# Inverting the softmax sums of the last node phase by logarithm, exponential and one Newton step instead of a division

## The chip, the cores and the metric

The kernel runs on one core of one Trainium2 chip. The time is device microseconds of one execution; the median of three runs stands for a kernel. The profile is of one more execution, taken by the hardware profiler. Engines are TensorE (PE, and PEld for its weight loads), VectorE (DVE), ScalarE (ACT), GpSimd (POOL) and SyncE (SP, which here issues DMAs).

## What is computed

A graph of 6250 nodes with 128 features passes through four layers (attention, a GIN-like layer, an equivariant layer, attention by feature), each followed by a residual sum and a layer norm. The change lies behind the last one, of which this is the core:

```python
a = f_src[src] + f_dst[dst]
e = jnp.where(a >= 0, a, NEG_SLOPE * a)
sa = _edge_softmax(e, dst, n)            # exp(e - max) / sum over the edges of a node
m = f_v[src] * sa
rst = jax.ops.segment_sum(m, dst, num_segments=n)
...
x = _layernorm(x + rst, axis=-1)         # (x - mean) / sqrt(var + 1e-5)
```

The division by the sum is the same for all edges of a node, so the kernel adds up exponentials and weighted exponentials and divides once per node and feature.

## The kernel before, in words

Nodes lie in 49 tiles of 128 (partition = node in the tile). `x` holds the features [128, 49, 128], `acc` the accumulators [128, 49, 384]. The program is a row of phases: a projection, then four times an edge phase (`edges0` to `edges3`: gather rows of both ends, compute messages, add them up by matrix multiplications with selection matrices, add to `acc`) and a node phase (`after0` to `after3`). A barrier over all engines stands between phases.

Behind `edges3`, `acc[:, tile, 0:128]` holds the sums of exponentials and `acc[:, tile, 128:256]` the weighted sums. `acc[:, tile, 256:384]`, which the program calls `side(tile)`, held one end's features for `edges3` and is not read any more.

`after3` (L736) handles 13 blocks of four tiles (128x512 numbers an instruction), the last one being a single tile. For a block it does:
- ScalarE, L749: the sum plus 1e-30, by an Identity with a bias column `tiny`, into `s`
- VectorE, L753: reciprocal of that, into `z`
- GpSimd, L757 and L760: times the weighted sums, plus `x`
- `layernorm` (L482): VectorE takes statistics of the four tiles (L487), aggregates them (L490), adds eps (L473, a tensor_scalar on 128x4 numbers); ScalarE takes the root (L477); VectorE the reciprocal (L480) and minus mean times that (L493); ScalarE writes the four tiles of the output by an activation with scale and bias (L500)
- SyncE, L766 and L769: the block's write-out.

Five streams work in turn, each with its own tiles and semaphores: stream k has blocks k, k+5, k+10. `node_phase` (L523) fixes the order of the instructions on every engine when the program is built: each step of a stream yields the engine it needs and a weight, and the loop always takes the step that could start first by those weights, the older block first among equals. On the chip the engines follow these lists in order and wait for each other by semaphores. `k.enter` makes the first instruction of a block on an engine wait for all that the stream's block before has done; `also` is a further chain of steps beside the streams, which `after3` doesn't use yet.

Of the kernel before, what the change touches and what calls it, by code (L numbers as in the profile page):

```python
# [15 lines left out]
P = 128  # L16
N_NODES = 6250
N_EDGES = 106250
D = 128
BLOCK = 4  # L20
STREAMS = 4
X_TILES = 12
N_TILES = -(-N_NODES // P)
# [8 lines left out]
N_BLOCKS = -(-N_TILES // BLOCK)  # L32
# [17 lines left out]
ALU = mybir.AluOpType  # L50
ACT = mybir.ActivationFunctionType
# [31 lines left out]
def wait(engine, *marks):  # L83

    last = {}
    for counter, at in marks:
        last[counter] = max(at, last.get(counter, 0))
    for counter, at in last.items():
        engine.wait_ge(counter.sem, counter.round * counter.per + (counter.base + at))
# [62 lines left out]
def build(nc, a):  # L152
    PE, V, A, G, SP = nc.tensor, nc.vector, nc.scalar, nc.gpsimd, nc.sync
# [26 lines left out]
    def sb(ctx, name, shape, dt=F32):  # L180
        return ctx.enter_context(nc.sbuf_tensor(name, shape, dt))


    x = sb(root, "x", [P, N_TILES, D])
    acc = sb(root, "acc", [P, N_TILES, ACC_W])
# [16 lines left out]
    def side(tiles):  # L202

        return acc[:, tiles, SIDE:SIDE + D]
# [7 lines left out]
    def counters(ctx):  # L212
        return lambda name, by=1: Counter(ctx.sem(name), by)
# [187 lines left out]
    def sliced(t, k):  # L401

        return t[:, 0:k.size]
# [119 lines left out]
    def node_phase(tag, make, n_streams=STREAMS, also=None, begin=0.0):  # L523

        with Phase(nc, tag) as ctx:
            def blocks(k, steps):
                for b in range(k.number, N_BLOCKS, n_streams):
                    k.start(b)  # L530
                    yield from steps()

            def age(s):
                return chained[s].first if chained[s] else -1

            streams = [Stream(ctx, s, n_streams) for s in range(n_streams)]
            chained = [None] * bool(also) + streams
            closing = []
            chains = ([also(ctx, closing)] if also else []) + [blocks(k, make(k)) for k in streams]
            upcoming = [next(chain) for chain in chains]  # L540
            chain_free, engine_free = [0.0] * bool(also) + [begin] * n_streams, {e: 0.0 for e in ENGINES}
            while any(upcoming):
                at, _, s = min((max(chain_free[s], engine_free[step[0]]), age(s), s)
                               for s, step in enumerate(upcoming) if step)
                engine, weight = upcoming[s]
                engine_free[engine] = at + weight
                chain_free[s] = at + weight + HAND_OVER
                upcoming[s] = next(chains[s], None)
            for k in streams:
                for e in ENGINES:  # L550
                    wait(e, *[(c, c.at) for c in (k.pe, k.v, k.act, k.g, k.out) if c.at])
            for e in ENGINES:
                wait(e, *closing)
            ctx.end()
# [179 lines left out]


    def after3():  # L736
        def make(k):
            z, s = (k.sb(n, [P, BLOCK, D]) for n in ("z", "s"))
            y, tiny = k.sb("y", [P, BLOCK, D]), k.sb("tiny", [P, 1])

            def steps():
                if k.first == k.number * BLOCK:
                    yield V, 0.1
                    m_tiny = k.v.did(V.memset(tiny[:], 1e-30))
                yield A, 0.7
                k.enter(A)
                if k.first == k.number * BLOCK:
                    wait(A, m_tiny)
                m = k.act.did(A.activation(sliced(s, k), acc[:, k.own, 0:D], ACT.Identity, bias=tiny[:]))  # L749
                yield V, 3.3  # L750
                k.enter(V)
                wait(V, m)
                m = k.v.did(V.reciprocal(sliced(z, k), sliced(s, k)))  # L753
                yield G, 1.4
                k.enter(G)
                wait(G, m)
                m = k.g.did(G.tensor_tensor(sliced(z, k), sliced(z, k), acc[:, k.own, D:2 * D], ALU.mult))  # L757
                yield G, 1.4
                wait(G, m)
                m = k.g.did(G.tensor_tensor(sliced(z, k), sliced(z, k), x[:, k.own, :], ALU.add))  # L760
                m = yield from k.layernorm(z, lambda j: y[:, j, :], [m])
                yield SP, 0.4
                wait(SP, m)
                whole = min(k.size, FULL_TILES - k.first)
                if whole:
                    k.out.did(SP.dma_start(a["out"][k.first * P:(k.first + whole) * P, :]  # L766
                                           .rearrange("(t p) d -> p t d", p=P), y[:, 0:whole, :]))
                if whole < k.size:
                    k.out.did(SP.dma_start(a["out"][FULL_TILES * P:N_NODES, :], y[0:REST, whole, :]))  # L769
            return steps  # L770
        node_phase("after3", make, 5)


    class EdgePass:
# [802 lines left out]
    with root:  # L1577
        project0()
        edges0()
        after0()  # L1580
        edges1()
        after1()
        edges2()
        after2()
        edges3()
        after3()
# [48 lines left out]
```

## Time and profile before

| | us |
|---|---|
| median of three runs (lowest, highest) | 5061.64 (5058.72, 5064.53) |
| the profiled execution | 5061.25 |
| its span, first to last instruction | 5059.5 |
| VectorE busy over the span | 3631.7 (72%) |
| GpSimd busy | 3588.2 (71%) |
| TensorE busy | 3558.8 (70%) |
| ScalarE busy | 2794.9 (55%) |

The span is what the profiler sees between the first and the last instruction. An engine is busy while an instruction of its own is under way, whatever that instruction waits for after it has been started; so a busy time can hold waits. A row of the order of time gives start, duration, engine, line, operation, the tile written and the tiles read, the shape where all have one, and the count of instructions put together in the row. Tile names have their phase cut down (`after_z`, `e_rows`), so a line number tells which phase a row belongs to.

### The profile page before, as it was taken

What the parts mean: (1) busy time and instruction counts of PE and PEld (TensorE: products, weight loads), DVE (VectorE), ACT (ScalarE), POOL (GpSimd) and SP (SyncE); (2) the same over time, 40 slices, a digit from 0 to 9 for tenths busy, and PEclk for the clock granted to TensorE, in tenths of its full rate; (3) what the DMA queues carried; (4) which work ended last, traced back from release to release, by engine and by line L of the source; (5) the groups of instructions that cost most, each with busy time, mean ns of one, the idle gap of its engine ahead of it and who ended that gap; (6) DMA issues with size and microseconds to landing.
All of it is one profiled execution on the core that took longest, in us unless ns stands there. A gap on an engine that the chain in (4) does not pass through costs nothing. (4 is left out here: it accounts for less than half of the span.)

```text
span 5059.5 us, 96093 instructions
## 1 busy us (share of the span) xinstructions
PE 3558.8 (70%) x20064; PEld 2945.0 (58%) x20065; DVE 3631.7 (72%) x8845; ACT 2794.9 (55%) x7180; POOL 3588.2 (71%) x3861
## 2 busy tenths in 40 slices
PE   5445444542476666666688888888779999999993
PEld 4444444442365555555566666666667777777772
DVE  5666666667654444444787777777679999999998
ACT  2444444444622222222576666666558888888885
POOL 4777777775677777776277777777548877777773
PEclk8777777776687777777789999999899999999997
DMA  6544444442433333332022112122157767766662
GB/s 186 157 156 156 156 156 156 156 156 87 122 84 79 80 80 80 80 80 73 28 68 57 56 56 57 56 56 57 38 147 195 191 189 189 190 188 190 189 190 55
DMA packets 491118, 596.80 MB, mean 118 GB/s; under 512 B 127483, under 2 KB 349165, under 8 KB 490639
## 3 DMA queue, kind: packets, MB, share of 16 engines
q0 software_dynamic: 141696, 349.47, 24.9%
q1 hardware_dynamic: 348463, 245.90, 16.9%
q10 hardware_dynamic: 864, 0.39, 0.1%
q8 instruction: 32, 0.52, 0.0%
q14 instruction: 63, 0.52, 0.0%
HBM read 505.89 MB, written 30.07 MB: 106 GB/s over the span
## 5 line engine op out<-in xcount | busy, mean ns | idle before, releaser
L917 DVE TENSOR_TENSOR acc<-acc,banks 128x256 f32 (+1 forms) x3520 | 1346.2, 382 | 599.8 <-PE banks L893 410.1
L893 PE MATMUL banks<-e_rows,e_sel 128*128 128x256 f32 x3520 | 961.2, 409 | 110.4 <-DVE acc L917 105.1
L832 POOL DMA_INDIRECT e_rows<-fsv_t,e_index x820 | 815.7, 995 | 246.9 <-issue 246.9
L832 POOL DMA_INDIRECT e_rows<-kv_t,e_index x820 | 789.9, 963 | 249.7 <-issue 245.5
L832 POOL DMA_INDIRECT e_rows<-x_t,e_index x820 | 774.7, 945 | 257.1 <-issue 243.2
L832 POOL DMA_INDIRECT e_rows<-up_t,e_index x820 | 774.6, 945 | 249.9 <-issue 207.3
L868 ACT ACTIVATE e_away<-node_iota,local 128x128 f32<-128x128 f32 x2640 | 837.0, 387 | 8.4 <-issue 1.9
L893 PEld LDWEIGHTS banks<-e_rows,e_sel 128*128 128x128 f32 x3520 | 663.4, 204 | 253.2 <-DVE acc L917 166.4
L893 PE MATMUL banks<-e_msg,e_sel 128*128 128x137 f32 (+1 forms) x3520 | 756.8, 364 | 7.4 <-DVE acc L917 3.4
L994 PE MATMUL banks<-acc,e_sel_t 128*128 x1760 | 314.4, 334 | 566.9 <-DVE e_sel_t L961 551.9
L1131 ACT ACTIVATE e_rows<-banks,e_rows 128x128 f32<-128x128 f32 x880 | 251.4, 370 | 775.0 <-PE banks L1122 374.0
L893 PEld LDWEIGHTS banks<-e_msg,e_sel 128*128 128x128 f32 x3520 | 620.3, 217 | 55.7 <-DVE acc L917 3.8
L994 PEld LDWEIGHTS banks<-acc,e_sel_t 128*128 128x128 f32 x1760 | 273.7, 237 | 602.7 <-issue 602.4
L1122 PE MATMUL banks<-e_w,e_attr 65*128 65x128 f32 x1760 | 288.9, 317 | 380.0 <-DMA e_attr<-in_attr_rows 379.9
L1122 PEld LDWEIGHTS banks<-e_w,e_attr 65*128 65x128 f32 x1760 | 274.9, 228 | 414.6 <-issue 363.3
L876 ACT ACTIVATE e_sel<-e_away,ones_col 128x512 f32<-128x512 f32 x660 | 473.6, 718 | 21.0
L1024 ACT ACTIVATE e_msg<-e_clip 128x32 f32<-128x32 f32 x220 | 51.1, 232 | 627.7 <-DVE e_clip L1019 627.7
L961 DVE TENSOR_SCALAR e_sel_t<-e_near,node_step 128x512 f32<-128x512 f32 x220 | 111.9, 509 | 323.1 <-DMA e_near<-near_d 322.7
L1289 ACT ACTIVATE e_h<-banks,e_b 64x256 f32<-64x256 f32 x440 | 206.9, 470 | 211.6 <-PE banks L1298 208.5
L1298 PE MATMUL banks<-e_w,e_h 65*128 65x128 f32 x1760 | 253.0, 289 | 97.4 <-DVE e_msg L1350 96.8
L1298 PEld LDWEIGHTS banks<-e_w,e_h 65*128 65x128 f32 x1760 | 229.5, 198 | 151.5 <-issue 127.1
L1487 DVE TENSOR_TENSOR_SCAN e_top<-banks,e_top,e_logit 128x512 f32<-128x512 f32 x220 | 280.8, 1276 | 5.8 <-PE banks L1474 3.4
(209 smaller groups left out, 6438.0 us busy)
## 6 DMA issues: line engine op xcount, KB each, us to landing
e_near<-near_d SPq DMA_DIRECT2D x440, 258.0 KB, 4.4
e_far<-acc SPq DMA_DIRECT2D x880, 64.0 KB
e_attr<-in_attr_rows SPq DMA_DIRECT2D x880, 32.0 KB
e_rows<-kv_t,e_index POOLq DMA_INDIRECT x820
e_rows<-x_t,e_index POOLq DMA_INDIRECT x820
e_rows<-up_t,e_index POOLq DMA_INDIRECT x820, 2.5
e_rows<-fsv_t,e_index POOLq DMA_INDIRECT x820
kv_t<-proj_kv SPq DMA_DIRECT2D x12, 512.0 KB
```

What stands on the lines that cost most here:

```text
L832: G.indirect_dma_start(out=self.rows[:, u, i, 0:self.width], out_offset=None, in_=self.table, in_offset=bass.IndirectOffsetOnAxis(ap=index ...
L868: m = A.activation(away[:, i, :], node_iota[:], ACT.Abs, bias=local[:, ds(g.n * GROUP + i, 1)], scale=-1.0)
L876: A.activation(self.place_of_sel(g), away[:], ACT.Relu, bias=ones_col[:], scale=-1.0).then_inc(self.s_sel, 1)
L893: m = PE.matmul(bank[n_bank][:, col + at:col + at + rows.shape[1]], self.place_of_sel(g)[:, i, :], rows, start=True, stop=True)
L917: V.tensor_tensor(to, to, bank[n_bank][:, col:col + self.sums].unsqueeze(1), ALU.add).then_inc(self.s_added[i], 1)
L961: V.tensor_scalar(self.sel_t[:, g.r2], self.near[:, g.at(self.nears), :, 1:], node_step[:], None, ALU.is_equal).then_inc(self.s_t, 1)
L994: m = PE.matmul(bank[B_Q[g.r2]][:, i * P:(i + 1) * P], by_node.sel_t[:, g.r2, i, :], side(ds(tiles[i], 1)).rearrange("p a d -> p (a d)"), ...
L1122: m = PE.matmul(bank[B_H[g.r2]][:, i * P:(i + 1) * P], attr[:, g.at(SPAN), i, :], w1[:], start=True, stop=True)
L1131: m = A.activation(ps.row(g)[:, i, D + 1:], bank[B_H[g.r2]][:, i * P:(i + 1) * P], ACT.Relu, scale=ps.row(g)[:, i, 0:1])
L1289: m = A.activation(h2[0:RH, g.r2, h * 2 * P:(h + 1) * 2 * P], hidden_bank(g, 1)[units, :], ACT.Silu, bias=b1[units, :])
L1298: m = PE.matmul(bank[B_W[g.r2]][:, i * P:(i + 1) * P], h2[:, g.r2, i * P:(i + 1) * P], w2[:], start=True, stop=True)
L1487: V.tensor_tensor_scan(top[:, g.at(SPAN), :], bank[B_R], logit[:, g.at(SPAN), :], top_before(g), ALU.add, ALU.max).then_inc(s_run, 1)
```

## The change

The first three blocks (`DIRECT = 3`) are still divided, now by a negation on VectorE and a reciprocal. For the other ten, ScalarE computes all logarithms of the sums in a row and then all of exp(-log) in a row, at the start of the phase, into `side`. VectorE makes one step of Newton's from this start value y: first (sum + 1e-30) * y, then (that - 2) * y, which is minus the improved inverse. The sign is taken up by GpSimd, which now subtracts the product from `x` instead of adding it. There are six streams instead of five, the tile `s` is gone, and the logarithms and exponentials are the further chain `also`.

```diff
     def after3():
+        inverted, DIRECT = [], 3
+
+        def inverses(ctx, closing):
...
+            make = counters(ctx)
+            v, act = make("v_i"), make("act_i")
+            tiny = ctx.sb("tiny", [P, 1])
+            m_tiny = v.did(V.memset(tiny[:], 1e-5))
+            blocks = [slice(b * BLOCK, min((b + 1) * BLOCK, N_TILES)) for b in range(DIRECT, N_BLOCKS)]
+            yield A, 0.65 * len(blocks)
+            wait(A, m_tiny)
+            ready = [act.did(A.activation(side(own), acc[:, own, 0:D], ACT.Ln, bias=tiny[:])) for own in blocks]
+            yield A, 0.65 * len(blocks)
+            for own, m in zip(blocks, ready):
+                wait(A, m)
+                inverted.append(act.did(A.activation(side(own), side(own), ACT.Exp, scale=-1.0)))
+            closing.append(m_tiny)
+
         def make(k):
...
-                yield A, 0.7
-                k.enter(A)
...
-                m = k.act.did(A.activation(sliced(s, k), acc[:, k.own, 0:D], ACT.Identity, bias=tiny[:]))
-                yield V, 3.3
-                k.enter(V)
-                wait(V, m)
-                m = k.v.did(V.reciprocal(sliced(z, k), sliced(s, k)))
...
+                if k.first < DIRECT * BLOCK:
+                    yield V, 3.9
+                    k.enter(V)
+                    m = k.v.did(V.tensor_scalar(sliced(z, k), acc[:, k.own, 0:D], -1.0, -1e-30, ALU.mult, ALU.add))
+                    wait(V, m)
+                    m = k.v.did(V.reciprocal(sliced(z, k), sliced(z, k)))
+                else:
+                    yield V, 1.5
+                    k.enter(V)
+                    wait(V, inverted[k.first // BLOCK - DIRECT])
+                    m = k.v.did(V.scalar_tensor_tensor(out=sliced(z, k), in0=acc[:, k.own, 0:D], scalar=1e-30,
+                                                       in1=side(k.own), op0=ALU.add, op1=ALU.mult))
+                    wait(V, m)
+                    m = k.v.did(V.scalar_tensor_tensor(out=sliced(z, k), in0=sliced(z, k), scalar=2.0, in1=side(k.own),
+                                                       op0=ALU.subtract, op1=ALU.mult))
                 yield G, 1.4
                 k.enter(G)
                 wait(G, m)
                 m = k.g.did(G.tensor_tensor(sliced(z, k), sliced(z, k), acc[:, k.own, D:2 * D], ALU.mult))
                 yield G, 1.4
                 wait(G, m)
-                m = k.g.did(G.tensor_tensor(sliced(z, k), sliced(z, k), x[:, k.own, :], ALU.add))
+                m = k.g.did(G.tensor_tensor(sliced(z, k), x[:, k.own, :], sliced(z, k), ALU.subtract))
                 m = yield from k.layernorm(z, lambda j: y[:, j, :], [m])
...
-        node_phase("after3", make, 5)
+        node_phase("after3", make, 6, inverses)
```

With the weights the order of the instructions changes too. First ScalarE's list from the start of the last phase, as it was (the number behind a tile's name is the stream):

```order
L749 ACTIVATE after3_s0<-acc,after3_tiny0 128x512
L749 ACTIVATE after3_s1<-acc,after3_tiny1 128x512
L749 ACTIVATE after3_s2<-acc,after3_tiny2 128x512
L749 ACTIVATE after3_s3<-acc,after3_tiny3 128x512
L749 ACTIVATE after3_s4<-acc,after3_tiny4 128x512
L477 ACT_TABLE_LOAD
L477 ACTIVATE after3_small0<-after3_small0 128x4
L500 ACTIVATE after3_y0<-after3_z0,after3_small0 128x128 x4
```

and as it is now:

```order
L750 ACT_TABLE_LOAD
L750 ACTIVATE acc<-acc,after3_tiny 128x4x128 x9
L750 ACTIVATE acc<-acc,after3_tiny 128x128
L754 ACT_TABLE_LOAD
L754 ACTIVATE acc<-acc 128x4x128 x9
L754 ACTIVATE acc<-acc 128x128
L477 ACT_TABLE_LOAD
L477 ACTIVATE after3_small0<-after3_small0 128x4
L500 ACTIVATE after3_y0<-after3_z0,after3_small0 128x128 x4
```

All logarithms and exponentials, and three table loads, now stand ahead of the root of block 0. VectorE's list of the new program, from the memset that opens the phase to the first block with a Newton step (L765 is the negation, L767 the reciprocal, L772 and L775 the two instructions of the step):

```order
L746 MEMSET after3_tiny 128x1
L765 TENSOR_SCALAR after3_z0<-acc 128x512
L767 RECIPROCAL after3_z0<-after3_z0 128x512
L765 TENSOR_SCALAR after3_z1<-acc 128x512
L767 RECIPROCAL after3_z1<-after3_z1 128x512
L487 BN_STATS after3_stats0<-after3_z0 128x6 x4
L490 BN_AGGR after3_mean_var0<-after3_stats0 128x2 x4
L765 TENSOR_SCALAR after3_z2<-acc 128x512
L767 RECIPROCAL after3_z2<-after3_z2 128x512
L473 TENSOR_SCALAR after3_small0<-after3_mean_var0 128x4
L487 BN_STATS after3_stats1<-after3_z1 128x6 x4
L490 BN_AGGR after3_mean_var1<-after3_stats1 128x2 x4
```

Behind these stand the reciprocal, the L493 and the L473 that follow the roots of blocks 0 and 1, and then, block after block, this piece (here the step of stream 4's second block, block 10):

```order
L772 SCALAR_TENSOR_TENSOR after3_z4<-acc 128x512
L775 SCALAR_TENSOR_TENSOR after3_z4<-after3_z4,acc 128x512
L487 BN_STATS after3_stats3<-after3_z3 128x6 x4
L490 BN_AGGR after3_mean_var3<-after3_stats3 128x2 x4
L480 RECIPROCAL after3_small2<-after3_small2 128x4
L493 SCALAR_TENSOR_TENSOR after3_small2<-after3_mean_var2,after3_small2 128x4
L473 TENSOR_SCALAR after3_small3<-after3_mean_var3 128x4
L772 SCALAR_TENSOR_TENSOR after3_z5<-acc 128x512
```

The statistics of a block stand behind the step of the next block, and the operations after its root behind the step of the one after that; before, a division stood in the place of the step.

## Rows read from the trace of the kernel before

**Rows 1.** Busy time by stretch, us and counts; the stretch of the last phase.
```profile
core 0: us, PE busy (x) PEld busy (x) DVE busy (x) ACT busy (x) POOL busy (x), PEclk, DMA share, GB/s
...
4991.00:5060.00 69.00, 0.00 (x0) 0.00 (x0) 58.63 (x155) 31.90 (x76) 31.19 (x26) 0.50 0.16 47
```

**Rows 2.** Groups by line, last phase: busy us, mean ns, idle before.
```profile
L753 DVE RECIPROCAL after_z<-after_s 128x512 f32<-128x512 f32 x12 | 39.9, 3334 | 0.7 <-ACT after_s L749 0.7
...
L757 POOL TENSOR_TENSOR after_z<-after_z,acc 128x512 f32<-128x512 f32 x12 | 15.2, 1264 | 40.7 <-DVE after_z L753 40.7
L760 POOL TENSOR_TENSOR after_z<-after_z,x 128x512 f32<-128x512 f32 x12 | 15.2, 1263 | 0.9
```

**Rows 3.** Order of time, two blocks of the steady state.
```profile
5023.21 3.35 DVE L753 RECIPROCAL after_z<-after_s 128x512 f32<-128x512 f32 x1
...
5026.72 0.87 DVE L487 BATCH_NORM_STATS2 after_stats<-after_z 128x6 f32<-128x128 f32 x4
5026.74 1.27 POOL L757 TENSOR_TENSOR after_z<-after_z,acc 128x512 f32<-128x512 f32 x1 [2.23 <-DVE after_z L753]
...
5027.62 0.38 DVE L490 BATCH_NORM_AGGREGATE after_mean_var<-after_stats 128x2 f32<-128x6 f32 x4
5027.91 3.32 DVE L753 RECIPROCAL after_z<-after_s 128x512 f32<-128x512 f32 x1
5028.08 1.26 POOL L760 TENSOR_TENSOR after_z<-after_z,x 128x512 f32<-128x512 f32 x1
...
5032.71 3.35 DVE L753 RECIPROCAL after_z<-after_s 128x512 f32<-128x512 f32 x1
```

**Rows 4.** Order of time, start of the last phase to the fourth division.
```profile
4991.07 3.17 ACT L749 ACTIVATE after_s<-acc,after_tiny 128x512 f32<-128x512 f32 x5 [12.30 <-DVE after_tiny L744]
...
5002.82 0.20 ACT L477 ACTIVATE after_small<-after_small 128x4 f32<-128x4 f32 x1 [7.28 <-DVE after_small L473]
...
5004.22 3.35 DVE L753 RECIPROCAL after_z<-after_s 128x512 f32<-128x512 f32 x1
```

**Rows 5.** First node phase in order of time, and L662 (after1), ns min/median/max.
```profile
1227.48 1.29 POOL L631 TENSOR_TENSOR after_t<-x,b2e 128x512 f32<-128x512 f32 x1
1227.55 1.24 DVE L473 TENSOR_SCALAR after_small<-after_mean_var 128x4 f32<-128x4 f32 x1
...
1235.55 1.64 POOL L620 TENSOR_TENSOR after_z<-after_z,x 128x512 f32<-128x512 f32 x1 [0.70 <-DVE after_z L614]
...
1235.99 1.75 DVE L614 TENSOR_TENSOR after_z<-acc,after_zs 128x512 f32<-128x512 f32 x1
...
L662 DVE SCALAR_TENSOR_TENSOR after_h<-after_z,inv_root_deg,acc x49: 337/346/1361, 2411.3 to 2496.5; 128x128 f32<-128x128 f32 x49
```

**Rows 6.** Nearest operations: by line ns min/median/max; L692 by order of time.
```profile
L1467 DVE SCALAR_TENSOR_TENSOR e_logit<-banks,e_logit x220: 665/683/691, 3745.4 to 4966.7; 128x512 f32<-128x512 f32 x110
...
L614 DVE TENSOR_TENSOR after_z<-acc,after_zs x13: 628/679/1747, 1217.4 to 1263.6; 128x512 f32<-128x512 f32 x12, 128x128 f32<-128x128 f32 x1
...
2427.27 1.13 DVE L692 SCALAR_TENSOR_TENSOR after_z<-after_xb,after_small,x 128x128 f32<-128x128 f32 x4
...
L961 DVE TENSOR_SCALAR e_sel_t<-e_near,node_step x220: 465/482/728, 87.2 to 1190.3; 128x512 f32<-128x512 f32 x110
...
L684 ACT ACTIVATE after_sq<-after_z x13: 297/620/641, 2421.8 to 2513.3; 128x512 f32<-128x512 f32 x12, 128x128 f32<-128x128 f32 x1
```

**Rows 7.** ScalarE in order of time, a table load in the phase edges1.
```profile
1302.50 1.28 ACT L1174 ACT_TABLE_LOAD   x1
1303.80 1.06 ACT L1174 ACTIVATE e_emb<-e_emb 128x1024 f32<-128x1024 f32 x1
```

**Rows 8.** Order of time, the last block's division and the last activations.
```profile
5046.91 0.92 DVE L753 RECIPROCAL after_z<-after_s 128x128 f32<-128x128 f32 x1
...
5052.26 2.03 ACT L500 ACTIVATE after_y<-after_z,after_small 128x128 f32<-128x128 f32 x5 [0.41 <-DVE after_small L493]
```

More of the change, by code:

```diff
@@ L737, in make @@
         def make(k):
-            z, s = (k.sb(n, [P, BLOCK, D]) for n in ("z", "s"))
-            y, tiny = k.sb("y", [P, BLOCK, D]), k.sb("tiny", [P, 1])
+            z, y = (k.sb(n, [P, BLOCK, D]) for n in ("z", "y"))
             def steps():
-                if k.first == k.number * BLOCK:
-                    yield V, 0.1
-                    m_tiny = k.v.did(V.memset(tiny[:], 1e-30))
-                yield A, 0.7
-                k.enter(A)
-                if k.first == k.number * BLOCK:
-                    wait(A, m_tiny)
-                m = k.act.did(A.activation(sliced(s, k), acc[:, k.own, 0:D], ACT.Identity, bias=tiny[:]))
-                yield V, 3.3
-                k.enter(V)
-                wait(V, m)
-                m = k.v.did(V.reciprocal(sliced(z, k), sliced(s, k)))
+                if k.first < DIRECT * BLOCK:
[13 more added lines that the diff above has]
+                                                       op0=ALU.subtract, op1=ALU.mult))
```

## The prediction, made before the changed kernel ran

> **What bounds the kernel now.** I read the busy times by stretch first. The change touches only the last phase, 69 of 5059.5 us. In it TensorE does nothing, VectorE is busy 58.6 us, ScalarE 31.9 and GpSimd 31.2 [rows 1]. The groups of that phase say what VectorE does: twelve divisions of a whole block take 39.9 us, 3.33 us each; GpSimd's multiplication takes 1.26 us and its addition as much [rows 2]. The order of time shows the rhythm: divisions start at 5023.21, 5027.91 and 5032.71, so a block takes 9.50 / 2 = 4.75 us. Of this 3.3 us is the division, and 1.45 us the rest: statistics 0.90 us to the next instruction, aggregation 0.30 us, three small operations together about 0.3 us. GpSimd starts 0.18 us after a division ends (5026.56 to 5026.74), starts its second operation 1.34 us after the first and is done at 5029.34, long before the next division ends [rows 3]. ScalarE needs 4 x 0.41 us for a block's outputs (five in 2.03 us [rows 8]) and 0.2 us for the root [rows 4]. So VectorE alone sets the pace, and a shorter inversion should pay until something else does.
>
> **What else could set it.** VectorE and GpSimd can't both work on every pair of instructions. In the first node phase GpSimd began an addition of 1.29 us at 1227.48; VectorE's 128x4 operation at 1227.55 took 1.24 us and ended as GpSimd's did. It goes the other way too: GpSimd's addition at 1235.55 took 1.64 us instead of 1.26, behind a VectorE instruction, and VectorE's next one, at 1235.99, took 1.75 us instead of 0.68. The 128x128 form of the very instruction that the change adds, with both tensors in SBUF, takes 346 ns as a rule and 1361 ns at worst [rows 5]. The division has one input and runs beside GpSimd at 3.32 to 3.35 us whatever GpSimd does [rows 3]. So the change replaces an instruction that shares with one that doesn't.
> The Trainium skill (SBUF — State Buffer, Who interferes with whom) has this as a rule: VectorE with two SBUF inputs and a GpSimd instruction that reads SBUF take turns at one shared port, for whole instructions. By that rule, the trace agrees (1.24 us for an operation of 0.1 us), this change gains little.
>
> **Prices.** The added STT of 128x512 (scalar_tensor_tensor) is not in the trace in its form. Nearest: the same operation with one input in PSUM, 683 ns; a two-tensor product from SBUF, 628 ns at least and 679 ns median; four STTs of 128x128 from SBUF, together 1.13 us, dearer for their four starts [rows 6]. I take 0.68 us, ends 0.63 and 1.13. The small block's STT: 0.34 us [rows 5]. The negation before a direct division: 0.48 us [rows 6]. Ln has a bias column like the Identity now: five take 3.17 us [rows 4], so (3.17 - 0.72) / 4 = 0.61 us each; Exp without one like the Square, 0.62 us, overlapping to 0.52 [rows 6]. A table load takes 1.28 us, and the next activation starts 1.30 us after its start [rows 7].
> The Trainium skill (ScalarE: Activation LUTs, What ACT_TABLE_LOAD costs) gives 2.66 us a switch, the drain of the engine included. The row disagrees, and the sum goes by the row; by the page the sum would be a rival below.
>
> **The steady state, term by term.** In the new order VectorE runs, for each block: STT, STT, statistics and aggregation of the block before, then reciprocal, small STT and small tensor_scalar. GpSimd gets a block after its second STT. Each STT excludes GpSimd, so the cycle is what must take turns: 0.68 + 0.68, 0.04 between them for the dependence (an estimate from the small operations' spacing), 0.18 to GpSimd's start, 1.26 + 0.08 + 1.26, less about 0.05 as VectorE starts the moment GpSimd stops: **4.15 us** (4.05 with STTs of 0.63, 5.05 with 1.13). The 1.2 us of statistics and aggregation lie beside GpSimd's multiplication, and the small STT falls between GpSimd's two operations. Without taking turns the cycle would be VectorE's own sum, 1.36 + 0.90 + 0.30 + about 0.34 = 2.9 us, with GpSimd's 2.7 close under it. GpSimd's subtraction has the form and price of the addition. ScalarE's 1.85 us a block and the write-outs, one in 4.15 us instead of 4.75, stay hidden; the sixth stream only gives a block's buffers more time.
>
> **The start.** Now ScalarE's Identity is at 4991.07, block 0's root runs at 5002.82 and the fourth division starts at 5004.22 [rows 4]. After the change VectorE does, from 4991.0: negation and division twice, 7.6 us, to 4998.6; statistics and aggregation of block 0, 1.2 us, to 4999.8; negation, 0.3 us of it behind GpSimd, and the third division, to 5003.9; statistics and aggregation of block 1, to 5005.2. Then it needs block 0's root. ScalarE does first: load 1.3, nine Ln 5.5 and the small one 0.4, load 1.3, nine Exp 4.7 and the small one 0.3, load 1.3, root 0.2, together 15.0 us, to 5006.0. So VectorE, which now waits for nobody there, waits 0.8 us; its small STT then meets GpSimd's subtraction of block 2, up to 0.7 us more. The first STT of the fourth block starts about 5006.8: **2.6 us late**. What hides ScalarE's 15 us is the three direct divisions; without them it would be on the path in full. Ln and Exp of a Newton block are long done when it comes.
>
> **The sum.** From the fourth block to the small last one the profile has 5004.22 to 5046.91, 42.7 us [rows 4, 8]. After: one interval of 2.9 us, since GpSimd has no backlog yet, and eight of 4.15, 33.2: 36.1 us, **6.6 us less**. The tail now takes 7.4 us (5046.91 to 5054.29) [rows 8]: 0.92 us of division goes, two STTs of 0.34 and a wait of up to 1.2 us behind GpSimd come, part of which the following statistics would have waited anyway: **+0.2**. The last write-out behind it, 5.2 us to the end of the span, is as before. Net 2.6 - 6.6 + 0.2 = **-3.8 us**. The profiled execution took 5061.25 us: 5057.45 after. The median of the runs is 5061.64, 0.4 above it, so I forecast **5057.8 us**.
> A measurement of this kernel can tell about 0.2%, 10.1 us, from no change: faster is below 5051.5, slower above 5071.8.
>
> **Rivals.**
> 1. No turns for the large STTs. The 2.9 us cycle holds: 9 x 2.9 = 26.1 instead of 42.7, a start only 1.9 us late: -14.5 us, 5047. For it: an STT of 512 elements is nowhere in the trace beside GpSimd, and of 49 small ones more than half took the bare 346 ns. Against: 1361 ns for one with both inputs in SBUF, with GpSimd at work. Chance 0.11.
> 2. Slower: nothing overlaps. The mechanism is that statistics wait for the GpSimd operation of the block just handed over, or hold the port too, so that a cycle is the whole chain: 1.40 + 0.18 + 2.60 + 0.90 + 0.30 + 0.34, about 5.7 us. 9 x 5.7 = 51.3 instead of 42.7, with start and tail +11.4: 5073. It decides from a cycle of 4.75 + (10.1 - 2.8) / 9 = 5.56 us. Against it: the order puts statistics of the block before behind the STTs, and in the profile statistics at 5026.72 and GpSimd's multiplication at 5026.74 both keep their bare times [rows 3]. Chance 0.04.
> 3. Dear table switches. If ScalarE needed 1.38 us more at each of three loads, the root would come 4.1 us later, and the start 3.6 us later beside the small wait that this swallows: 5061.4, no change to speak of. That is the page's 2.66 us. Against it: 1302.50 to 1303.80 [rows 7]. Chance 0.07.
> 4. STTs at their dear end, 1.13 us: 9 x 0.9 = +8 on the forecast, 5066. Chance 0.05.
> The forecast's own case keeps 0.73.
>
> **How the numbers follow.** Faster by over 0.2%: rival 1 and a little of the forecast's lower edge, 0.13. Slower by over 0.2%: rival 2 and 0.01 of mishap, 0.05. The rest, 0.82, is within 0.2%. The forecast with cycles of 4.05 to 4.3 us and the runs' own scatter of 3 us to either side spans 5053 to 5062; taking in rival 3 and most of the way to rivals 1 and 4, the range is **5049 to 5064**.
>
> **What the profile would show.** Right: three divisions; in the steady state an STT pair that starts every 4.1 to 4.2 us, one of the two at 0.68 us and the other at 1.8 to 1.9 us with GpSimd's subtraction inside it; VectorE nearly always "busy" although it waits; three table loads; block 0's root at about 5006; the outputs' last activation ending near 5050.5. Wrong: both STTs at 0.68 us and a cycle near 2.9 (rival 1); GpSimd idle during statistics and a cycle over 5.5 (rival 2); the root after 5009 (rival 3); a difference that lies outside the last phase, where the change has no instruction.

## The result, and the profile after

The changed kernel takes 5054.46 us (median of 19 runs, 5051.48 to 5058.54), the kernel before 5063.22 us (19 runs, 5058.72 to 5066.19), run beside it. The ratio is 0.9983, with a 95% interval of 0.9976 to 0.9990: 8.8 us less. That is a small gain clear of the scatter, and below the 0.2% (10.1 us) that the prediction calls a change, though the interval reaches 0.24%. It is inside the predicted range, 3.3 us under the 5057.8 us of the forecast. The profiled execution took 5054.69 us; its span is 5052.9 us.

Everything that the change does lies in the last phase, and its length repeats far better than the whole time does: from VectorE's first instruction in it to the end of the last output activation it is 63.31 us before (4990.98 to 5054.29) and 56.34 us after (4991.96 to 5048.30), and a second profile of the changed kernel has 56.35. "The phase" means this stretch from here on, and a time "in the phase" is counted from its start. Where it went, beside the prediction's terms:

| | before | after | difference | forecast |
|---|---|---|---|---|
| start to the fourth block's first instruction | 13.24 | 15.35 | +2.1 | +2.6 |
| fourth block to the small last one (nine intervals) | 42.69 | 33.61 | −9.1 | −6.6 |
| small block to the last activation's end | 7.38 | 7.38 | 0.0 | +0.2 |
| the phase | 63.31 | 56.34 | −7.0 | −3.8 |

The busy times of the phase after (the counterpart of [rows 1]; columns as there):

```profile
4991.90:5048.30 56.40, 0.00 (x0) 0.00 (x0) 50.64 (x164) 36.22 (x85) 35.18 (x26) 0.50 0.18 52
```

and its groups by line and shape (the counterpart of [rows 2]):

```profile
L783 POOL TENSOR_TENSOR after_z<-x,after_z 128x512 f32<-128x512 f32 x12 | 19.0, 1586 | 0.9
L780 POOL TENSOR_TENSOR after_z<-after_z,acc 128x512 f32<-128x512 f32 x12 | 15.2, 1270 | 29.8 <-DVE after_z L767 21.8 <-DVE after_z L775 7.9
L775 DVE SCALAR_TENSOR_TENSOR after_z<-after_z,acc 128x512 f32<-128x512 f32 x9 | 12.8, 1427 | 0.3
...
L767 DVE RECIPROCAL after_z<-after_z 128x512 f32<-128x512 f32 x3 | 10.1, 3353 | 0.1
L772 DVE SCALAR_TENSOR_TENSOR after_z<-acc 128x512 f32<-128x512 f32 x9 | 7.3, 806 | 0.0
```

Nine large divisions are gone and three are left. Of Newton's two instructions, the first (L772) has a mean of 806 ns, the second (L775) 1427, for the same shape and the same number of operands: seven of the nine second ones take 1.64 us, and one of the first ones 1.75 us. Its partner is in the first row: GpSimd's subtraction (L783) has a mean of 1586 ns, where the addition that it replaces had 1263 [rows 2], while the multiplication (L780) kept its time. VectorE counts as busy for 50.64 us, and part of that is waiting inside instructions. Two blocks of the steady state in order of time show it:

```profile
5025.59 0.69 DVE L772 SCALAR_TENSOR_TENSOR after_z<-acc 128x512 f32<-128x512 f32 x1
...
5025.63 1.78 POOL L783 TENSOR_TENSOR after_z<-x,after_z 128x512 f32<-128x512 f32 x1
5026.31 1.64 DVE L775 SCALAR_TENSOR_TENSOR after_z<-after_z,acc 128x512 f32<-128x512 f32 x1
...
5027.87 0.86 DVE L487 BATCH_NORM_STATS2 after_stats<-after_z 128x6 f32<-128x128 f32 x4
5028.12 1.26 POOL L780 TENSOR_TENSOR after_z<-after_z,acc 128x512 f32<-128x512 f32 x1 [0.72 <-DVE after_z L775]
...
5029.42 0.69 DVE L772 SCALAR_TENSOR_TENSOR after_z<-acc 128x512 f32<-128x512 f32 x1
5029.46 1.77 POOL L783 TENSOR_TENSOR after_z<-x,after_z 128x512 f32<-128x512 f32 x1
```

The cycle is 29.42 − 25.59 = 3.83 us, where [rows 3] had 4.75. Read it by ends. GpSimd's subtraction needs 1.26 us when nothing disturbs it and ends at 27.41, that is 1.26 + 0.56 us after L772 started, not 1.26 + 0.69. L775 was issued at 26.31 and ended at 27.95, 0.54 us after GpSimd did. So the two engines take turns, and a turn of the large two-tensor instruction on VectorE adds about 0.54 to 0.56 us, not its whole 0.69. Added up by turns the cycle is 0.56 + 1.26 + 0.54 + 0.17 to GpSimd's start + 1.26 + 0.04 = 3.83.

VectorE's own list gives the same 3.83, and says more. From L775's end (5027.95) to the next L772 (5029.42) VectorE works through statistics, aggregation and small operations without a wait, 1.47 us, and GpSimd's multiplication fits beside them. The only wait of VectorE in the cycle is inside L775: 1.64 − 0.69 = 0.95 us, for GpSimd's subtraction. So the cycle is VectorE's own 2.88 us and this one wait; that the turns add up to the same is a tie. The kernel below with its subtraction on VectorE tells the two apart.

The start of the phase, ScalarE's list and VectorE behind it (the counterpart of [rows 4]):

```profile
4991.89 1.28 ACT L750 ACT_TABLE_LOAD   x1 [12.14 <-PEq L110]
...
4993.19 5.91 ACT L750 ACTIVATE acc<-acc,after_tiny 128x512 f32<-128x512 f32 x10
...
4999.12 1.28 ACT L754 ACT_TABLE_LOAD   x1
...
5000.41 4.99 ACT L754 ACTIVATE acc<-acc 128x512 f32<-128x512 f32 x10
...
5005.41 1.28 ACT L477 ACT_TABLE_LOAD   x1
5005.88 1.26 POOL L783 TENSOR_TENSOR after_z<-x,after_z 128x512 f32<-128x512 f32 x1
5006.71 0.21 ACT L477 ACTIVATE after_small<-after_small 128x4 f32<-128x4 f32 x1
5006.95 0.18 DVE L480 RECIPROCAL after_small<-after_small 128x4 f32<-128x4 f32 x1 [1.28 <-ACT after_small L477]
5007.16 0.16 DVE L493 SCALAR_TENSOR_TENSOR after_small<-after_mean_var,after_small 128x4 f32<-128x4 f32 x1
```

ScalarE works 15.0 us without a gap and VectorE waits 1.28 us for it. The small instruction at 5007.16 then did not wait, since GpSimd's subtraction had just ended (5007.14).

The end of the phase (the counterpart of [rows 8]):

```profile
5040.92 0.29 DVE L772 SCALAR_TENSOR_TENSOR after_z<-acc 128x128 f32<-128x128 f32 x1
5040.96 1.37 POOL L783 TENSOR_TENSOR after_z<-x,after_z 128x512 f32<-128x512 f32 x1
...
5041.24 1.24 DVE L775 SCALAR_TENSOR_TENSOR after_z<-after_z,acc 128x128 f32<-128x128 f32 x1
...
5046.27 2.03 ACT L500 ACTIVATE after_y<-after_z,after_small 128x128 f32<-128x128 f32 x5 [0.41 <-DVE after_small L493]
```

A turn of the small block's instruction is shorter in proportion: GpSimd was done at 5042.33, 1.26 + 0.15 us after the 0.29 us instruction had started, and L775 at 5042.48, 0.15 us after GpSimd.

### The profile page after: what moved, and what is told of

It reads as the page before. It is cut to its first block and busy times, and to the rows that moved or that the text cites. A ratio compares the mean times of both kernels' runs of the same rounds, so it can differ in the third digit from the quotient of the medians.

```text
span 5052.9 us, 96126 instructions
## 1 busy us (share of the span) xinstructions
PE 3550.7 (70%) x20064; PEld 2935.0 (58%) x20065; DVE 3620.5 (72%) x8854; ACT 2799.0 (55%) x7189; POOL 3593.9 (71%) x3861
```

## The experiments

Theory: VectorE's instructions with two tensors in SBUF and GpSimd's exclude each other, and the rest of the phase follows from that and from ScalarE's 15 us at the start. Rivals: the second instruction is slow because it depends on the first; the statistics or the small operations set the cycle; the start is set by dearer table switches.

The first four kernels ran on a chip on which the phases before the last took about 30% longer (the kernel before took 6575.37 us there). The instructions of the last phase kept their durations (the same 0.69 and 1.26 us), so only the phase is compared for these four.

**Start values in PSUM.** The exponentials of blocks 3 to 10 go to the eight PSUM banks, unused at this time, those of 11 and 12 stay in SBUF. Newton's step is the same, but each instruction now has one input in SBUF and one in PSUM:

```diff
+        def start_of(tiles):
+            b = tiles.start // BLOCK - DIRECT
+            if b >= 8:
+                return side(tiles)
+            return bank[b][:, 0:(tiles.stop - tiles.start) * D].rearrange("p (t d) -> p t d", d=D)
...
-                inverted.append(act.did(A.activation(side(own), side(own), ACT.Exp, scale=-1.0)))
+                inverted.append(act.did(A.activation(start_of(own), side(own), ACT.Exp, scale=-1.0)))
...
-                                                       in1=side(k.own), op0=ALU.add, op1=ALU.mult))
+                                                       in1=start_of(k.own), op0=ALU.add, op1=ALU.mult))
...
-                    m = k.v.did(V.scalar_tensor_tensor(out=sliced(z, k), in0=sliced(z, k), scalar=2.0, in1=side(k.own),
+                    m = k.v.did(V.scalar_tensor_tensor(out=sliced(z, k), in0=sliced(z, k), scalar=2.0, in1=start_of(k.own),
```

> The changed kernel, but exp(-log) of blocks 3 to 10 is written to the eight PSUM banks, so that both STTs of those blocks have one SBUF input only; blocks 11 and 12 stay in SBUF. Work, order and counts are the same. Port theory (an STT with two SBUF inputs and a GpSimd operation take turns, which makes the cycle of 3.84 us): STTs at 0.68 to 0.70 us beside GpSimd, GpSimd's subtraction back at 1.26 us instead of 1.78, cycle of blocks 4 to 10 near VectorE's own 2.9 to 3.1 us, the last phase 5 to 6 us shorter than the 56.3 us it takes in the changed kernel. Dependence theory (the statistics wait for GpSimd's subtraction, whatever the ports do): cycle stays at 3.8 us, phase 56 us.

Measured: a phase of 49.60 us, pairs at 15.34, 18.19, 21.03, 23.91 us and so on, 2.88 us apart in the mean, up to block 10; behind block 11, whose start value is in SBUF, the interval is 3.84 again. The port theory's expectation is met, with a somewhat larger gain than it had (6.7 us of phase). The whole time is told from a second run of this kernel on a chip of the usual speed, with the unchanged kernel of the change as a control beside it.

> The changed kernel itself, run again so that the other kernels of this call have it on the same chip. Last phase 56.3 us and cycle 3.84 us as in its first profile; ratio to the kernel before 0.998 to 0.999.

> The version with the start values of blocks 3 to 10 in PSUM again, now timed. Its last phase took 49.6 us in one look against 63.3 before and 56.3 in the changed kernel. If nothing else differs, 13.7 + 0.6 us less than before, ratio 0.997 to 0.9975, and about 6.7 us less than the changed kernel.

Measured: control 5060.35 us, ratio to before 0.9985 (0.9976 to 0.9994); start values in PSUM 5053.35 us, ratio 0.9969 (0.9957 to 0.9981), phase 49.59 us: 7.0 us less than the control in the whole time, 6.8 in the phase. Its order of time, one block of the steady state and then block 11:

```profile
5020.40 1.27 POOL L789 TENSOR_TENSOR after_z<-x,after_z 128x512 f32<-128x512 f32 x1
5020.45 0.69 DVE L778 SCALAR_TENSOR_TENSOR after_z<-acc,banks 128x512 f32<-128x512 f32 x1
...
5021.18 0.69 DVE L781 SCALAR_TENSOR_TENSOR after_z<-after_z,banks 128x512 f32<-128x512 f32 x1
...
5023.34 0.69 DVE L778 SCALAR_TENSOR_TENSOR after_z<-acc,banks 128x512 f32<-128x512 f32 x1
...
5034.91 0.69 DVE L778 SCALAR_TENSOR_TENSOR after_z<-acc 128x512 f32<-128x512 f32 x1
5034.95 1.78 POOL L789 TENSOR_TENSOR after_z<-x,after_z 128x512 f32<-128x512 f32 x1
...
5035.63 1.64 DVE L781 SCALAR_TENSOR_TENSOR after_z<-after_z,acc 128x512 f32<-128x512 f32 x1
```

The second instruction depends on the first in both blocks; it takes 0.69 us beside a working GpSimd when one input is in PSUM, and 1.64 us when both are in SBUF. That settles the cause of the long L775 and rules out the dependence. The stretch from the second instruction's end to the next first one is 1.47 us here too (5021.87 to 5023.34). It is also the fastest kernel of this study that computes all of the change's arithmetic: 6.8 us of phase less than the change, 13.7 less than before.

**The subtraction on VectorE.**

```diff
-                yield G, 1.4
-                wait(G, m)
-                m = k.g.did(G.tensor_tensor(sliced(z, k), x[:, k.own, :], sliced(z, k), ALU.subtract))
+                if k.first < DIRECT * BLOCK:
...
+                else:
+                    yield V, 0.7
+                    wait(V, m)
+                    m = k.v.did(V.tensor_tensor(sliced(z, k), x[:, k.own, :], sliced(z, k), ALU.subtract))
```

> The changed kernel with the subtraction from x of the ten Newton blocks moved from GpSimd to VectorE (0.68 us instead of 1.26). Port theory: the turns shrink to 1.26 + 3 x 0.54 + 0.3 for hand-overs = 3.2 us, VectorE's own sum grows to 2.9 + 0.6 = 3.5 us and now sets the cycle: 3.5 to 3.7 us, phase 54 to 55 us. If GpSimd's operations did not cost VectorE anything, VectorE would only get more work and the cycle would grow from 3.84 to 4.4 us, phase 61 us.

Measured: a phase of 58.59 us, with pairs at 15.36, 18.81, 22.70, 29.27, 30.60, 34.86 us: neither expectation. The new weight moved VectorE's order about, so that twice two pairs of steps stand 1.3 us apart behind an interval of 6.6 us. This kernel changed two things at once and decides nothing. Its repair keeps every list in the order of the change and only puts the subtraction directly ahead of the block's statistics:

> The change with GpSimd's subtraction moved to VectorE, in front of the block's statistics, and every list otherwise in the order of the change. If a block's 3.84 us is VectorE's own work plus one turn of GpSimd's of 1.26 us for each of its two operations that meets a combined operation, the block costs 1.36 + 0.04 + 0.61 + 0.90 + 0.30 + 0.34 = 3.55 us and the last phase is near 54 us. If GpSimd's operations cost VectorE nothing in the steady state, the block gets 0.61 us longer, 4.45 us, and the phase is near 61.5 us.

Measured: 54.23 us, a steady cycle of 3.61, close to the 3.55 us and 54 us of the first expectation. In order of time:

```profile
5022.22 0.69 DVE L775 SCALAR_TENSOR_TENSOR after_z<-acc 128x512 f32<-128x512 f32 x1
...
5022.95 0.69 DVE L778 SCALAR_TENSOR_TENSOR after_z<-after_z,acc 128x512 f32<-128x512 f32 x1
5023.56 0.68 DVE L792 TENSOR_TENSOR after_z<-x,after_z 128x512 f32<-128x512 f32 x1
...
5023.81 1.55 POOL L783 TENSOR_TENSOR after_z<-after_z,acc 128x512 f32<-128x512 f32 x1 [2.06 <-DVE after_z L778]
...
5024.27 0.87 DVE L490 BATCH_NORM_STATS2 after_stats<-after_z 128x6 f32<-128x128 f32 x4
...
5025.83 0.69 DVE L775 SCALAR_TENSOR_TENSOR after_z<-acc 128x512 f32<-128x512 f32 x1
```

VectorE does 0.6 us more for each block, and the block takes 0.2 us less. GpSimd has only its multiplication left, which falls beside the statistics; here VectorE waits for nobody and 3.61 us is its own sum. From the start of the statistics (L490 here) to the next first instruction it is 1.56 us, though the multiplication was over 0.47 us before; in the changed kernel, where it ends just ahead of that instruction, it is 1.55 us (5027.87 to 5029.42). So the multiplication costs VectorE nothing in the change, and its turn is no part of what sets the pace; the subtraction's is. The multiplication ends at 5025.36, that is 1.26 + 0.54 us after the start of the two-tensor subtraction of 0.68 us: the same short turn.

**A division for every block, with the negation kept.** `DIRECT = N_BLOCKS`, six streams: the change's negation and subtraction without its logarithms.

> The changed kernel with all 13 blocks divided directly (negation on VectorE, then reciprocal), no logarithms or exponentials, six streams. It is the kernel before with the Identity of ScalarE replaced by a negation of 0.45 us on VectorE. If VectorE alone sets the pace there, the cycle is 4.75 + 0.4 = 5.15 us and the last phase 63.3 + 12 x 0.4 - 0.3 = 67.8 us. If the negation, which takes turns with GpSimd, also waits for GpSimd, 5.3 us or more and 70 us. If six streams by themselves gain something, below 67.

Measured: a phase of 71.55 us, 8.2 us longer than the kernel before; blocks are (64.39 − 0.46) / 12 = 5.33 us apart instead of 4.75. The negation has a mean of 578 ns over its thirteen. Two of them take 1.51 us, and they stand behind GpSimd's subtraction; this is one:

```profile
6521.15 1.26 POOL L783 TENSOR_TENSOR after_z<-x,after_z 128x512 f32<-128x512 f32 x1
6521.19 1.51 DVE L765 TENSOR_SCALAR after_z<-acc 128x512 f32<-128x512 f32 x1
```

So the negation, which has one tensor input, waits behind GpSimd as well. The division does not, at 3.35 us each time. The phase grew by 8.2 us, of which the thirteen negations are 7.5; 70 us or more was the expectation for a negation that waits, and the two long ones make up 2.2 us of it.

**Newton for every block.** First with `DIRECT = 0`, the streams planned to start 9 us into the phase:

> The changed kernel with DIRECT = 0: all 13 blocks by Newton. The prediction's view, that the three direct divisions hide ScalarE's 15 us and that without them it would be on the path in full: the last phase 10 us or more longer than 56.3 us. Rival view, that only the order root after exponentials counts: the first STT can start at 11 us from the phase's start (load, 13 logarithms, load, one exponential), block 0's root at 17 us, the first STT of the fourth block about 17.3 us instead of 15.35, and the phase is only about 2 us longer, 58.3 us.

Measured: 65.13 us. That is between the two expectations. The order made when the program is built has five pairs of steps ahead of the first statistics, with the first four 2.3 us apart or less and later ones up to 6.9, so start and order are mixed and it decides little. Its repair keeps the lists of the change and replaces the three divisions by Newton's step:

```diff
-            blocks = [slice(b * BLOCK, min((b + 1) * BLOCK, N_TILES)) for b in range(DIRECT, N_BLOCKS)]
+            blocks = [slice(b * BLOCK, min((b + 1) * BLOCK, N_TILES)) for b in range(N_BLOCKS)]
...
-                if k.first < DIRECT * BLOCK:
...
-                    m = k.v.did(V.tensor_scalar(sliced(z, k), acc[:, k.own, 0:D], -1.0, -1e-30, ALU.mult, ALU.add))
-                    wait(V, m)
-                    m = k.v.did(V.reciprocal(sliced(z, k), sliced(z, k)))
-                else:
+                if True:
```

> All 13 blocks by Newton, and every engine's list as in the changed kernel, with the two STTs in the place of each of the three divisions. It asks what the three direct divisions hide, without the changed order that DIRECT = 0 brought. Prediction's view (they hide ScalarE's 15 us, which would be on the path in full otherwise): phase 10 us or more above 56.3. Rival view (the first STT can start at 11 us, block 0's root at 17 to 18 us, and what comes after that is the same): first STT of the fourth block at 18 to 20 us instead of 15.35, phase 59 to 61 us.

Measured: one run of 5063.63 us, and a phase of 62.93 us, hardly less than the 63.31 before. Again this is between the two expectations. The fourth block starts at 21.95 us in the phase, not at 15.35, and from there on all is as in the change. In order of time:

```profile
5005.23 0.69 DVE L767 SCALAR_TENSOR_TENSOR after_z<-acc 128x512 f32<-128x512 f32 x1 [10.88 <-ACT acc L755]
...
5010.09 0.87 DVE L487 BATCH_NORM_STATS2 after_stats<-after_z 128x6 f32<-128x128 f32 x4 [1.16 <-POOL after_z L778]
...
5013.73 0.20 ACT L477 ACTIVATE after_small<-after_small 128x4 f32<-128x4 f32 x1 [1.31 <-DVE after_small L473]
```

VectorE idles 10.88 us until the first exponential; the rest of ScalarE's list runs beside the first steps, and block 0's root, now at 19.44 us, waits for VectorE's statistics and no longer for the list. Idling and three Newton blocks take 10.9 + 11.0 us, where the three divided blocks with their wait take 15.35. So the three divisions are worth 6.6 us, not ScalarE's whole 15.

**Three divisions or four.** With start values in PSUM, `DIRECT = 4`:

> The kernel with start values in PSUM, with four direct divisions in place of three, so that only the last block's start value is in SBUF. A direct block more costs 4.6 to 5.2 us, and a block with its start value in SBUF less gives 3.84 us back; VectorE's wait of 1.28 us for ScalarE's first root should go. If three divisions leave ScalarE late, the phase is 49 to 50 us, the same as the 49.6 us with three. If the wait stays or the fourth division meets GpSimd's turns, it is 51 us or more.

Measured: 52.01 us, 2.4 more than with three, as the second expectation had it. The wait for the first root is gone, but:

```profile
5010.75 1.26 POOL L789 TENSOR_TENSOR after_z<-x,after_z 128x512 f32<-128x512 f32 x1
5010.89 1.14 DVE L493 SCALAR_TENSOR_TENSOR after_small<-after_mean_var,after_small 128x4 f32<-128x4 f32 x1
...
5019.97 1.28 POOL L789 TENSOR_TENSOR after_z<-x,after_z 128x512 f32<-128x512 f32 x1
5020.04 1.24 DVE L473 TENSOR_SCALAR after_small<-after_mean_var 128x4 f32<-128x4 f32 x1
```

The small instruction behind the root now meets GpSimd's subtraction and takes 1.14 us instead of 0.16, which eats the wait that was saved. The first Newton step comes 5.0 us later, and the missing block gives only 2.6 back (26.85 to 24.27 us to the small one), since a second small instruction meets a subtraction behind that step (1.24 us instead of 0.16): the first interval is 4.02 us, not 2.85. These two waits are 2.1 of the 2.4 us; without them a fourth division would be about even, which no run here shows.

**Two table loads more.** Logarithms and exponentials in two halves of five blocks:

```diff
-            ready = [act.did(A.activation(side(own), acc[:, own, 0:D], ACT.Ln, bias=tiny[:])) for own in blocks]
...
+            for half in (blocks[0:5], blocks[5:]):
+                ready = [act.did(A.activation(side(own), acc[:, own, 0:D], ACT.Ln, bias=tiny[:])) for own in half]
```

> The changed kernel with logarithms and exponentials in two halves (five logarithms, five exponentials, five, five), so two more table loads ahead of block 0's root and nothing else. At 1.29 us a switch the root comes 2.6 us later and so does the fourth block's first STT, phase 56.3 + 2.2 to 2.6 = 58.7 us. At 2.66 us a switch, the figure of the Trainium skill's page on ScalarE, root 5.3 us later and phase 61.3 us.

Measured: 5066.38 us, a phase of 59.20. Block 0's root comes at 17.59 us instead of 14.75, and the fourth block 2.84 us later. ScalarE in order of time, the two added loads:

```profile
5009.22 1.28 ACT L752 ACT_TABLE_LOAD   x1
5010.52 2.85 ACT L752 ACTIVATE acc<-acc,after_tiny 128x512 f32<-128x512 f32 x5
5013.39 1.28 ACT L755 ACT_TABLE_LOAD   x1
5014.68 2.39 ACT L755 ACTIVATE acc<-acc 128x512 f32<-128x512 f32 x5
```

Two loads cost 2 x 1.30 us from their start to the next activation's. The half lists together take 0.22 us more than the whole ones (3.17 + 2.85 against 5.91, 2.71 + 2.39 against 4.99), which is the rest. All of it lands on the phase: ScalarE's list is on the path at the start.

**The step left out.** Newton's step is left out for the ten late blocks: their inverse is exp(−log) alone (of the sum plus 1e-5, the bias `tiny`), in PSUM for blocks 3 to 10. VectorE multiplies the weighted sums by it, and GpSimd only adds `x`, so a GpSimd operation goes with the step.

```diff
-                    m = k.v.did(V.scalar_tensor_tensor(out=sliced(z, k), in0=acc[:, k.own, 0:D], scalar=1e-30,
-                                                       in1=side(k.own), op0=ALU.add, op1=ALU.mult))
-                    wait(V, m)
-                    m = k.v.did(V.scalar_tensor_tensor(out=sliced(z, k), in0=sliced(z, k), scalar=2.0, in1=side(k.own),
-                                                       op0=ALU.subtract, op1=ALU.mult))
+                    m = k.v.did(V.tensor_tensor(sliced(z, k), acc[:, k.own, D:2 * D], start_of(k.own), ALU.mult))
```

> This kernel leaves out Newton's step for the ten late blocks: there the inverse is exp(-log) alone, multiplied on VectorE with the weighted sums (start values of blocks 3 to 10 in PSUM, of 11 and 12 in SBUF), and GpSimd only adds x. It asks what the step itself costs. If VectorE is the bound as in the kernel with start values in PSUM (2.88 us a block, of which 0.68 us is the second combined operation), a block now costs about 2.2 us, and the last phase, 49.6 us there, is about 7 us shorter: 42 to 44 us. If ScalarE's 1.85 us a block, or GpSimd's chain, is a bound just behind VectorE, hardly anything is gained: 48 us or more.

Measured: 5046.65 us, ratio 0.9965 (0.9951 to 0.9979), a phase of 46.07 us, 3.5 less than with the step: between the two expectations. Two blocks take 5.5 us:

```profile
5025.18 0.65 DVE L778 TENSOR_TENSOR after_z<-acc,banks 128x512 f32<-128x512 f32 x1
...
5026.00 1.26 POOL L787 TENSOR_TENSOR after_z<-x,after_z 128x512 f32<-128x512 f32 x1 [2.10 <-DVE after_z L778]
5026.01 1.27 DVE L493 SCALAR_TENSOR_TENSOR after_small<-after_mean_var,after_small 128x4 f32<-128x4 f32 x1
...
5027.27 0.67 DVE L778 TENSOR_TENSOR after_z<-acc,banks 128x512 f32<-128x512 f32 x1
...
5030.71 0.65 DVE L778 TENSOR_TENSOR after_z<-acc,banks 128x512 f32<-128x512 f32 x1
```

One small instruction in every two blocks meets GpSimd's addition and takes 1.27 us instead of 0.16, and half of that, 0.55 us a block, is what separates 2.76 from the expected 2.2 us. An instruction on four elements a partition waits for GpSimd's whole operation as a large one does. Of the 3.5 us, about 2 fall at the end, behind the small block's instruction (5.43 us from there to the last activation's end instead of 7.39), and the rest in the nine intervals before.

**The sixth stream.** The kernel before with six streams instead of five:

> The kernel before with six streams in the last phase in place of five, the one part of the change that the division doesn't need. If the sixth stream is nothing by itself, the phase stays at 63.3 us within 0.3. If it hid waits, 62 us or less.

Measured: a phase of 63.27 us, where the kernel before has 63.31. The stream count is nothing by itself.

## Why the prediction was right

The forecast was no change beyond 0.2%, 5057.8 us, with the phase 3.8 us shorter; it is 7.0 us shorter, and the median 5054.46. By its own steps:

1. *VectorE alone set the pace, and a shorter inversion pays until something else does.* Right: the cycle fell from 4.75 to 3.83 us. What sets it now is VectorE's own list, 2.88 us, with one wait of 0.95 us for GpSimd's subtraction.
2. *The cycle of 4.15 us.* Taking turns was right and a size was off. The terms as written add up to 4.13. The sum charged each of the two large instructions for its whole 0.68 us. Their turn is 0.54 to 0.56 us, so the round is 3.83. [rows 5] already had this: the addition at 1235.55 ended at 1237.19 and VectorE's product of 0.68 us at 1237.74, 0.55 us behind it. The sum also counts the multiplication and its hand-overs as part of the cycle; they take 1.47 us beside 1.47 us of VectorE's own work, so it is by luck that this costs the sum nothing. Less than a third of a microsecond, but eight times: the nine intervals are 33.6 us, not 36.1, and this term carries 2.5 of the 3.2 us by which the phase was missed. Rival 1, no turns at all, has its cycle of 2.9 us where one input is in PSUM (2.88 us), and only there.
3. *The Trainium skill's rule* (SBUF — State Buffer, Who interferes with whom) has the port pair as an exclusive lock. The turns are there, as it says: 1.64 us for 0.69 on VectorE, 1.78 for 1.26 on GpSimd. Whether VectorE holds it for the whole instruction, as the prediction has it, the rows can't tell. The waiting VectorE instruction ends 0.54 us behind GpSimd's, and the waiting GpSimd operation 1.13 us behind VectorE's (5026.28 to 5027.41). So each engine has 0.13 to 0.15 us outside its turn, and a start-up that passes while it waits would look just so. The same section has it that an instruction with at most one SBUF input, outside the modes that use two ports, does not contend; Newton's two instructions with the start value in PSUM agree, at 0.69 us each beside GpSimd.
4. *The start, 2.6 us late.* It is 2.1. ScalarE's 15.0 us is exact (4991.89 to 5006.92). VectorE waited 1.28 us, more than the 0.8 forecast, since its own list was 0.5 us quicker; the charge of up to 0.7 us for a small instruction behind GpSimd's subtraction did not come in the change. It came as 1.14 us in the kernel with four divisions, so a matter of 0.02 us in the order of events decided it.
5. *"What hides ScalarE's 15 us is the three direct divisions; without them it would be on the path in full."* Wrong, though no term of the sum rests on it: without them the fourth block starts 6.6 us later. Only what stands ahead of the first exponential is then exposed.
6. *Rival 3, dear table switches.* Refuted. Each load delays the next activation by 1.29 to 1.30 us, in the change and in the kernel with two more. The Trainium skill (ScalarE: Activation LUTs, What ACT_TABLE_LOAD costs) gives 2.66 us with the drain; by an estimate from that figure the two added loads would have cost 5.3 us. They cost 2.84.
7. *The tail, +0.2.* It is 0.0.
8. *The last write-out, 5.2 us, as before.* It took 4.6 us in the profile after and 4.6 to 4.7 in every other kernel here, among them the division kernel with six streams (4.62). So the 5.2 us most likely belongs to that one profile of before, and isn't a gain of the change; there is no second profile of the kernel before to show it.

That leaves 8.8 us of difference between medians against 7.0 us of phase; the rest is no more than the last write-out and the runs' scatter can make (the ratio's interval is 5 to 12 us).

What stayed open: why the turn is shorter than the instruction. That a waiting VectorE instruction ends 0.54 us behind GpSimd, and a small one of 0.16 us only 0.02 us behind it (5012.01 to 5012.03 in the kernel with four divisions), says that about 0.14 us of it can pass while it waits. Whether a waiting GpSimd operation has such a part too, or VectorE gives way before its end, no run here separates.

## What to carry to other kernels

When a single long instruction that shares with GpSimd is replaced by two short ones with both inputs in SBUF, walk through both engines' lists and charge each wait where it falls, not the busy time of one: here 1.4 us in place of 3.35 brought 0.9 us a block. Look then for an input that may live in PSUM, since that took the turns away and gave another 0.95 us a block for a changed address. And a serial list on another engine at the start of a phase is hidden only by work that doesn't need it: count from its first result, not from its last, and try one block more and one less.

## What was not expected of the hardware

- A 128x512 scalar_tensor_tensor of 0.69 us from SBUF costs a round of turns only 0.54 to 0.56 us, a 128x128 one of 0.29 us 0.15, and a two-tensor subtraction of 0.68 us 0.54, if GpSimd's operation is counted with its full 1.26 us.
- Two dependent VectorE instructions back to back do not keep GpSimd out: its waiting subtraction got in between them, and the second then waited (L775, 1.64 us, in seven of nine large blocks). A subtraction issued 0.02 or 0.03 us ahead of the first instruction (at 5010.14 and 5013.94) still came second. Where GpSimd was first by 0.06 us, it was the first of the two that waited:

```profile
5017.74 1.26 POOL L783 TENSOR_TENSOR after_z<-x,after_z 128x512 f32<-128x512 f32 x1
5017.80 1.75 DVE L772 SCALAR_TENSOR_TENSOR after_z<-acc 128x512 f32<-128x512 f32 x1
...
5019.59 0.69 DVE L775 SCALAR_TENSOR_TENSOR after_z<-after_z,acc 128x512 f32<-128x512 f32 x1
```

- That order costs a little more: this interval is 3.95 us (25.84 to 29.79 in the phase) against 3.83 for the others.
